# A two-layer model on one core: the second layer's expert MLPs and state-space scans, reordered around wide decays and an accumulating DMA

## The reference

```
xn  = layernorm(x)
# state-space part, per feature h, with N = 16 states n
dt  = softplus(xn @ W_dt.T + b_dt)
state[h,n] = exp(dt * A[h,n]) * state[h,n] + dt * B[h,n] * xn[h]       # over the 512 tokens of a batch
y[h]       = sum_n C[h,n] * state[h,n] + D[h] * xn[h]                  # A = -exp(A_log)
# mixture of 64 experts of hidden size 32, the best 8 of each token
cw[e]  = normalized softmax weight of expert e, 0 where it isn't chosen
routed = sum_e cw[e] * (silu(xn @ w1[e] + b1[e]) @ w2[e] + b2[e])
shared = sum over 2 shared experts of silu(xn @ sw1 + sb1) @ sw2 + sb2
out    = x + y + routed + shared
```

## Time and profile before

| | |
|---|---|
| median of 3 runs | 551.22 us (550.59 to 553.37) |
| profiled execution, first to last instruction | 552.8 us |
| its mean granted TensorE clock | 0.945 |
| PE busy | 458.1 us (83%) |
| DVE busy | 432.0 us (78%) |
| ACT busy | 307.0 us (56%) |
| POOL busy | 228.2 us (41%) |
| DMA | 9.94 MB, mean 18 GB/s |

### The profile page before, as it was taken

The page is one execution under the profiler, slowest core; times in us unless marked ns, Lnnn a source line. Parts: engine busy times, 40 slices in busy tenths (PEclk is TensorE's granted clock), DMA queues, the critical chain, the costliest instruction groups (busy, mean ns, idle before and its releaser), DMA issues.

```text
span 552.8 us, 8403 instructions
## 1 busy us (share of the span) xinstructions
PE 458.1 (83%) x2143; PEld 325.5 (59%) x2143; DVE 432.0 (78%) x799; ACT 307.0 (56%) x491; POOL 228.2 (41%) x185
## 2 busy tenths in 40 slices
PE   2739999999999999999897875978877768686864
PEld 1427878888788887888676543544433434343431
DVE  6586588746886478945989685969999979799975
ACT  2375654346453574326442667367777657577750
POOL 2148014301422014400111009117887888788882
PEclk9969999999999999999999685899999989899987
DMA  6320000100110000000000000000000000000002
GB/s 178 80 66 14 2 17 24 42 0 0 39 42 7 0 0 0 0 0 1 0 2 1 0 1 1 1 0 5 14 14 9 14 5 19 9 9 19 5 2 76
DMA packets 24924, 9.94 MB, mean 18 GB/s; under 512 B 10325, under 2 KB 24902, under 8 KB 24902
## 3 DMA queue, kind: packets, MB, share of 16 engines
q1 hardware_dynamic: 24902, 9.69, 6.8%
HBM read 8.64 MB, written 1.05 MB: 18 GB/s over the span
## 4 chain that ended last, share of the span: by engine, by line
PE 29%; DVE 24%; POOL 24%; issue 11%; ACT 8%; POOLq 2%; DVEq 1%; DMA 1%; ACTq 0%; SPq 0%
POOL xn_tok L426 19%; PE psum L1097 7%; PE psum L193 6%; PE psum L195 6%; PE psum L194 6%; POOL g_hi L437 3%; PE psum L1217 2%; DVE hid L776 2%; DVE at_m L805 1%; DVE at_m L807 1%; POOL g_lo L438 1%; DVE xn_tok L698 1%; DVE res L857 1%; PE psum L1232 1%; DVE at_k L834 1%
## 5 line engine op out<-in xcount | busy, mean ns | idle before, releaser
L560 ACT ACTIVATE sil<-psum 128x512 f32<-128x512 f32 (+1 forms) x96 | 56.3, 596 | 104.3 <-PE psum L195 88.9
L776 DVE TENSOR_TENSOR hid<-sil,psum 128x512 f32<-128x512 f32 (+1 forms) x96 | 65.1, 686 | 51.8 <-PE psum L195 33.5
L1097 PEld LDWEIGHTS psum<-e_w,hid 128*128 128x128 f32 (+1 forms) x768 | 94.9, 191 | 5.9
L1097 PE MATMUL psum<-e_w,hid 128*128 128x128 f32 (+1 forms) x768 | 95.3, 274 | 0.0
L193 PE MATMUL psum<-xn_hi,e_hi 128*128 128x512 f32 (+1 forms) x192 | 81.5, 425 | 8.3 <-DVE hid L776 7.8
L195 PE MATMUL psum<-xn_lo,e_hi 128*128 128x512 f32 (+1 forms) x192 | 75.9, 395 | 0.0
L194 PE MATMUL psum<-xn_hi,e_lo 128*128 128x512 f32 (+1 forms) x192 | 75.6, 394 | 0.0
L193 PE MATMUL psum<-xn_hi,g_hi 128*128 128x512 f32 x64 | 36.5, 570 | 41.0 <-DVE hid L1001 23.9
L1269 PE MATMUL psum<-hid,g_w 128*128 128x512 f32 x128 | 68.7, 620 | 0.6 <-DVE hid L1001 0.6
L650 ACT ACTIVATE sil<-psum,b_half 128x512 f32<-128x512 f32 x64 | 43.7, 682 | 40.5 <-PE psum L195 40.5
L193 PEld LDWEIGHTS psum<-xn_hi,g_hi 128*128 128x128 f32 x64 | 12.6, 197 | 87.1 <-DVE hid L1001 81.2
(11 more groups left out here) (275 smaller groups left out, 944.7 us busy)
## 6 DMA issues: line engine op xcount, KB each, us to landing
e_raw<-in_L_ffn_w SPq DMA_DIRECT2D x16, 128.0 KB, 2.2
e_raw<-in_L_ffn_w SPq DMA_DIRECT2D x8, 176.0 KB, 2.5
res<-in_L_attn_x SPq DMA_DIRECT2D x4, 256.0 KB, 3.8
g_raw<-in_L_ffn_w SPq DMA_DIRECT2D x16, 64.0 KB, 2.0
g_w<-in_L_ffn_w SPq DMA_DIRECT2D x16, 64.0 KB, 1.8
out<-res SPq DMA_DIRECT2D x4, 256.0 KB, 2.4
e_raw<-in_L_ffn_w SPq DMA_DIRECT2D x16, 48.0 KB, 2.0
sw_raw<-in_L_ffn_sw SPq DMA_DIRECT2D x1, 256.0 KB, 3.0
```

The source lines that it names most:

```text
L560: act.activation(sil[0:M, s % 2, :], ps[s % 2][0:M, :], ACT.Silu).then_inc(silu_done, 1)
L776: dve.tensor_tensor(hid[0:M, tb % 2, ft, :], sil[0:M, s % 2, :], ps[2 + s % 2][0:M, :], ALU.mult).then_inc(gated, 1)
L1097: ins = pe.matmul(ps[4 + o % 2][:, n * P:(n + 1) * P], hid[0:m, tb % 2, ft, n * P:(n + 1) * P], e_w2[j][0:m, ft, :], start=(ft == 0), stop ...
```

## The change

In the routed stage:

- **Silu in one pass.** ACT applies Silu to `ps[s % 2]` with the bias b1 and DVE multiplies the result with the spread routing weights in one instruction. L1001, the halves of b1 and the factors of a half and of two go. PE's product now waits for ACT's Silu instead of DVE's second instruction.
- **Wide decays.** ACT makes the decay of a whole group (all four blocks) in one instruction; the first column of each block is left out and was set to zero by POOL once, so a scan can run over two blocks. Both decays of the next turn come at the end of a turn on ACT.
- **Wide scans.** DVE has four scans of 1024 elements in a turn instead of eight of 512, between the multiplications.
- **y by DMA.** ACT multiplies each half state (1024 elements) in place with B * C, and POOL issues a DMA that adds it to y in SBUF (`accum_op`). POOL's additions go. A scan waits until the DMA that reads its state buffer has landed, and a DMA until the earlier one on the same half of y has.
- The new buffers lie over buffers of the first layer; the loops of DVE and POOL over the turns are written out, those of ACT and PE stay loops.

```diff
@@ pool
+            pool.wait_ge(sp_exp, 1)
+            for j in range(GPI):
+                own(pool.memset(dec[j][:, :].rearrange("p (b t) -> p b t", t=TB)[:, :, 0:1], 0.0))
...
             def group_turn(i, last):
-                for s in range(GSTEPS):
-                    pool.wait_ge(weighted, i * GSTEPS + s + 1 + RING)
-                    own(pool.tensor_tensor(blk(y_t, tb), blk(y_t, tb), term_ring[s % RING][:, :], ALU.add))
-                    pool.nop().then_inc(y_added, 1)
...
+                for k in range(SCANS):
+                    pool.wait_ge(weighted, i * SCANS + k + 1)
+                    if i > 0 or k >= 2:
+                        pool.wait_ge(y_in[(k + 2) % SCANS], 16 * (i + k // 2))
+                    pool.dma_start(y_t[:, (k % 2) * HALF:(k % 2 + 1) * HALF], state[k][:, :], accum_op=ALU.add
+                                   ).then_inc(y_in[k], 16)
+                    if k % 2 == 1 and not last:
+                        split_next(i, k // 2)
@@ act
+            def decay(i, j):
+                act.wait_ge(scanned, i * SCANS + 2 * j + 2)
+                act.activation(dec[j][:, :].rearrange("p (b t) -> p b t", t=TB)[:, :, 1:TB],
+                               dt_t[:, :].rearrange("p (b t) -> p b t", t=TB)[:, :, 1:TB], ACT.Exp,
+                               scale=ssm_a[:, bass.ds(i * GPI + j, 1)]).then_inc(decay_ready, 1)
+            def weigh_state(i, k):
+                act.wait_ge(scanned, i * SCANS + k + 1 + SCANS)
+                act.activation(state[k][:, :], state[k][:, :], ACT.Copy,
+                               scale=ssm_cb[:, bass.ds(i * GPI + k // 2, 1)]).then_inc(weighted, 1)
             def group_turn(i, last):
                 for s in range(GSTEPS):
                     act.wait_ge(h_made, i * GSTEPS + s + 1)
-                    act.wait_ge(c1_done, i * GSTEPS + s + 1)
-                    act.activation(sil[:, s % 2, :], ps[s % 2][:, :], ACT.Tanh, scale=0.5,
-                                   bias=b1_half[:, bass.ds(g, 1)]).then_inc(tanh_done, 1)
+                    act.wait_ge(hid_done, i * GSTEPS + s + 1)
+                    act.activation(sil[:, s % 2, :], ps[s % 2][:, :], ACT.Silu,
+                                   bias=vec_t[:, bass.ds(g + V_B1, 1)]).then_inc(h_silu, 1)
+                    for k in range(SCANS):
+                        if s == min(2 * k + 2, GSTEPS - 1):
+                            weigh_state(i, k)
+                if not last:
+                    for j in range(GPI):
+                        decay(i + 1, j)
@@ dve
+            def scan(i, k):
+                dve.wait_ge(decay_ready, i * GPI + k // 2 + 1)
+                if i > 0:
+                    dve.wait_ge(y_in[k], 16 * i)
+                at_half = slice((k % 2) * HALF, (k % 2 + 1) * HALF)
+                dve.tensor_tensor_scan(state[k][:, :], dec[k // 2][:, at_half], win_t[:, at_half], 0.0,
+                                       ALU.mult, ALU.add).then_inc(scanned, 1)
+            def weigh(i, s):
+                c = i * GSTEPS + s
+                dve.wait_ge(h_silu, c + 3)
+                dve.wait_ge(cwx_made, c + 1)
+                dve.wait_ge(g_out, c + 1)
+                dve.tensor_tensor(hid_ring[s % 2], sil[:, s % 2, :], ps[2 + s % 2][:, :], ALU.mult
+                                  ).then_inc(hid_done, 1)
+            def group_turn(i):
+                weigh(i, 0)
+                for k in range(SCANS):
+                    scan(i, k)
+                    weigh(i, 2 * k + 1)
+                    if k + 1 < SCANS:
+                        weigh(i, 2 * k + 2)
@@ pe, expert_in
-                pe.wait_ge(hid_done, i * GSTEPS + s + 1)
+                pe.wait_ge(h_silu, i * GSTEPS + s + 1)
                 product(pe, ps[s % 2][:, :], g_hi[j][:, :], g_lo[j][:, :], blk(xn_hi, tb), blk(xn_lo, tb)
                         ).then_inc(h_made, 1)
-                pe.wait_ge(c1_done, i * GSTEPS + s + 1)
+                pe.wait_ge(hid_done, i * GSTEPS + s + 1)
                 pe.matmul(ps[2 + s % 2][:, :], sel_now[j][:, :], blk(cw_hl, tb), start=True, stop=True
```

More of the change, by code:

```diff
@@ L135, in program, with later @@
         e_w2_t = [sb(f"e_w2_t_{j}", [P, NF, P]) for j in range(2)]
+        span1 = nc.sbuf_base
+        def later(name, shape, offset):
+            assert offset + 4 * math.prod(shape[1:]) <= span1
+            return nc.alloc_sbuf_tensor_at(name, shape, F32, offset=offset)
+        dec_at = (span0 + 31) // 32 * 32
+        dec = [later(f"dec_{j}", [P, NTOK], dec_at + j * 4 * NTOK) for j in range(2)]
+        state = [later(f"state_{k}", [P, NTOK // 2], dec_at + 8 * NTOK + k * 2 * NTOK) for k in range(4)]
         sil = sb("sil", [P, 2, TB])
@@ L184, in program @@
         g_split, h_made, cwx_made = sem("g_split"), sem("h_made"), sem("cwx_made")
[L185 to L188, removed]
+        h_silu, hid_done, g_out = sem("h_silu"), sem("hid_done"), sem("g_out")
+        decay_ready, scanned = sem("decay_ready"), sem("scanned")
+        weighted = sem("weighted")
+        y_in = [sem(f"y_in{k}") for k in range(4)]
+        sum_ready, sum_turned, x2_ready = sem("sum_ready"), sem("sum_turned"), sem("x2_ready")
         def product(pe, acc, w_hi, w_lo, m_hi, m_lo):
@@ L216, in program @@
         hid_ring = [hid[:, r, 0, :] for r in range(2)]
[L217 to L221, removed]
+        HALF = NTOK // 2
+        SCANS = 2 * GPI
         softplus_bufs = [[at[n] for n in names] for names in (
@@ L604, in copy_cw @@
                     act.wait_ge(b2_used, b - 1)
-                act.activation(cw_b2[:, b % 2, :], ps[b % 2][0:E1, :], ACT.Copy, scale=2.0).then_inc(cw_copied, 1)
+                act.activation(cw_b2[:, b % 2, :], ps[b % 2][0:E1, :], ACT.Copy).then_inc(cw_copied, 1)
             for c in range(NSH * NBLK):
@@ L647, in group_turn @@
                     act.wait_ge(h_made, i * GSTEPS + s + 1)
-                    act.wait_ge(c1_done, i * GSTEPS + s + 1)
+                    act.wait_ge(hid_done, i * GSTEPS + s + 1)
                     act.nop().then_inc(act_passed, 1)
-                    act.activation(sil[:, s % 2, :], ps[s % 2][:, :], ACT.Tanh, scale=0.5,
-                                   bias=b1_half[:, bass.ds(g, 1)]).then_inc(tanh_done, 1)
[L652 to L661, removed]
+                    act.activation(sil[:, s % 2, :], ps[s % 2][:, :], ACT.Silu,
[6 more added lines that the diff above has]
+                        decay(i + 1, j)
+            act.nop().then_inc(h_silu, 2)
             act.wait_ge(win_ready, NBLK)
-            for s in range(2):
-                decay(0, s)
+            for j in range(GPI):
+                decay(0, j)
             with act.Fori(0, NG // GPI - 1) as i:
@@ L1004, in _ @@
-            scan(0, 0)
-            with dve.Fori(0, NG // GPI - 1) as i:
-                group_turn(i, False)
-            group_turn(NG // GPI - 1, True)
+            dve.nop().then_inc(scanned, SCANS)
+            def scan(i, k):
[5 more added lines that the diff above has]
+                                       ALU.mult, ALU.add).then_inc(scanned, 1)
@@ L1010, in _ @@
+            for i in range(NG // GPI):
+                group_turn(i)
             dve.wait_ge(g_out, NG * NBLK + 2)
-            dve.wait_ge(y_done, 1)
+            dve.wait_ge(y_in[2], 16 * (NG // GPI))
+            dve.wait_ge(y_in[3], 16 * (NG // GPI))
             for b in range(NBLK):
```

61 lines of the change are left out of this document (10 added, 51 removed).

## The result

The changed kernel takes 564.5 us (563.8 to 565.5), the kernel before 550.9 us: 2.3% more, ratio 1.0228 with a 95% interval of 1.0204 to 1.0253. It is slower, as forecast, but by 13.6 us and not by the 5.8 from 551.2 to 557.

A forecast was written before the change was run, and what follows sets the result against it. DVE, and POOL at turn ends, bound the routed stage. First fourth scan at 387.05, seven turns of 22.3, then weighting, DMA and hop: L1013 at 549.1 against 543.59, +5.5 on 551.2 gives 557 us; forecast range 553 to 563, wider range 542 to 576.

The forecast's parts named there:

- The mechanism: Routed stage: DVE gives back 5.4 us per turn, POOL's waits go, ACT's serial tail takes it all; 22.3 against 22.0.
- ACT's tail: Turn's end: weighting, load, two decays, load, Silu after DVE's fourth scan, 8.45 us; DVE starts at 8.64.
- Prices of instructions: New turn: wide scan 2.28 us, wide decay 1.99, half-state weighting 1.14, table load 1.30, Silu 0.69.
- a wait of 6.6 us will do the same or worse: PE's restart each turn: slow clock as after an earlier 3.02 us wait, output 4 at 18.3, turn 22.3 us.
- rival 3: Routed stage: scans stretched by POOL or clock low for two more steps, about +1.2 us per turn, 567; chance 0.13.
- The base of the sum: Whole kernel: +5.5 us from the profile added to the 551.2 median, taking the 552.8 profiled span as nearly the same.
- The start and the end: Stage's ends: last shared Silu at 366.03, first fourth scan at 387.05; finally weighting 1.29, DMA 4.5, hop 0.15, L1013 at 549.1.
- my own sign of being wrong: First half of the span (0 to 340 us): a change of over 1 us would show the forecast wrong.
- Rival 1: Routed stage: PE keeps its clock or DVE doesn't wait for it, 21.7 per turn, transfer lands in 3, 550.5; chance 0.13.
- Rival 2: ACT's tail: the two table loads per turn are not paid, tail shrinks by 2.6, 536 us; chance 0.13.
- Rival 4: Accumulating DMA is slow: at 15 us each a turn takes 30, total 625; decides from 11 us; chance 0.07.
- Rival 5: ACT's table loads: each also holds ACT up by its own 1.28 us, +20.5, 577; chance 0.04.

The follow-up runs named there:

- e10: Full change with both decays of a turn moved after that turn's own second Silu, same instructions and loads: 547.1 us, ratio 0.991 to the kernel before.
- e1: Full change with the decays computed by Silu in place of Exp, so no table loads in the stage: 538.4 us, ratio 0.974 to the kernel before.
- e2: Full change with PE repeating a routing matmul 28 times in its stop to keep its clock up: 556.1 us, ratio 1.0086 to the kernel before.
- e9: Full change with decays split up (four loads per turn), second and fourth weightings behind them, POOL's split ahead of those: 558.6 us, ratio 1.011 to kernel before.
- e3: Full change with the accumulating DMA moving only 32 of 1024 columns: 562.2 us, ratio 1.021 to the kernel before.
- e5: Kernel before with only POOL's additions replaced by accumulating DMAs, 64 of 256 KB: 533.5 us, ratio 0.968 to the kernel before.
- e8: Full change with next turn's decays after the fourth Silu (second buffer pair), plus 14 repeated PE matmuls in the stop: 537.0 us, ratio 0.973 to kernel before.

## Why the prediction was right in sign and wrong in size

- **The mechanism** stands. DVE gave back a third of its busy time, POOL's waits went, and ACT's tail in series took it all: 8.53 us from the fourth scan to DVE's next instruction against 8.64 forecast. e10, which moves this tail and nothing else, and e1, which shortens it, show it. What comes behind the tail was mis-sized.
- **Prices of instructions** were right: scan of 1024 2.28 (forecast 2.28), decay 1.99 (1.99), weighting 1.15 (1.14), load 1.29 (1.30), Silu 0.69.
- **The step that failed: "a wait of 6.6 us will do the same or worse".** I priced the restart as the one of the earlier trace rows and kept "or worse" for rival 3. That put the term at 0.6 us per turn (22.3 less DVE's 21.7); it measures 1.4 (23.17 less the 21.78 of e2). In detail: in six of seven turns PE stays at its lower level for 4.7 to 6.1 us; in the turn shown, with 5.7, output 4 is 1.04 us later than forecast, and the mean turn is 23.17 instead of 22.3. Over seven turns that is +6.1 us, and the largest part of the miss. The earlier trace rows was one case of a wait of 3.0 us; the changed kernel's turn of 22.1 us is another of that kind (2.9 us at 0.50) and fits the forecast, the others don't. e2 takes the restart away and lands on DVE's sum.
- **The base of the sum.** The profiled execution of before was a long one. In every run of the kernel before that was compared later, the time is 1.8 us above the span, so its span of 552.8 stands for some 554.6 us, while the median is 550.9. I had set its span equal to the median, "nearly the same", when it was 3.7 us above. Between the two profiled spans the change is +10.9 us (552.8 to 563.7); the span of before was 3.7 us longer than the median's and that of the changed kernel 1.0 (565.5 against 564.5), which is the other 2.7 of the 13.6.
- **The start and the end** nearly cancel: the last shared Silu ended 1.4 us earlier (364.64 against 366.03), which I had not forecast, and the first turn took 0.1 less than the sum; from the last scan to L1015 it took 0.2 more, 6.18 where 5.94 was taken (0.3 us pass between the weighting and POOL's issue), and what follows took 0.6 more. Together: 5.5 - 1.5 + 6.1 + 0.2 + 0.6 = 10.9. The earlier start meets my own sign of being wrong, a first part changed by over 1 us, but it isn't the change's: e2 and e9, which have the same instructions up to there, show that Silu's end at 366.34 and 366.29. From 310 to 320 us the granted clock was 0.78 in the profiles of before and of e2, and 0.99 in that of the changed kernel. That it hides 1.4 us of the miss is chance.
- **The rivals.** Rival 1 (PE doesn't matter, 21.7 per turn) is the turn of e2 and no turn of the changed kernel. Rival 2 (no loads) is what e1 makes, 538 against 536 worked out. Rival 3 had two halves. A clock that stays low for longer is what came in six of seven turns: +0.9 us per turn, where it had +1.2 and 567, so the result lies nearer to it than to the forecast. Scans stretched by POOL didn't come: the mean scan is 2.283 us. Rival 4 (slow DMA) is out at 4.7 us per transfer, and in e3 the turns are no shorter without the traffic. Rival 5 (a second cost beside each load) is out: 0.01 to 0.02 us on either side of the load in the timeline above. That was the drain of the Trainium skill ("ScalarE: Activation LUTs", What ACT_TABLE_LOAD costs), and this trace doesn't show it. The formula of the Trainium skill ("DMA: Bandwidth & Descriptors", Anatomy of one DMA, SWDGE path) for a POOL-issued transfer, an estimate of 3.2 us for 512 KB, is short of the 4.7 that this accumulating one took.

What stays open is what decides between 2.9 us of slow clock behind the stop and 6.1. The trace shows both behind the same 6.2 us of wait; it shows when the clock fell and rose, but not what set these moments, and no run here was made to separate them.

## What to carry to other kernels

When work is batched (one wide decay for a turn instead of eight narrow ones), ask what stands between the last consumer of the old batch and the first of the new one: a chain through two engines is paid in full, however idle both are on average. Put ahead of the batch whatever the next round can start with; here that one move was worth 17 us, the shorter stop of PE included. And price a stop of PE twice, by its length and by the slow matmuls behind it, from more than one case in the trace, and check what the profiled execution's own time is before adding to a median.

## What the runs showed of the hardware

- An accumulating DMA from SBUF to SBUF, issued by POOL: 512 KB (128 rows of 4 KB) land in 4.7 us, 256 KB in 3.2 to 3.5 (e5), 16 KB in 2.1 (e3). POOL is held 0.88 us by each issue, whatever the size, and DVE's fp32 scans beside it were not longer for the bytes it moves (mean 2.283 us with 512 KB, 2.284 with 16 KB).
- PE after a stop of 3.0 to 6.2 us mostly runs at a granted 0.50, for a time that varies: 2.9 to 6.1 us after seven equal stops of 6.2. Behind the repeats of e2 and e8, in place of the stop, it ran at 1.00.
- Equal stops of 3.9 us had two outcomes in e10. The one that ended at 395.08 was followed by 0.50 until 400.3; the one that ended at 416.04 by 1.00, then by 0.50 from 417.4 to 420.8.
